# Inverse roots as exp of minus half a logarithm, with one function table on ScalarE, in a kernel of two fused transformer layers

## The reference

```python
# layer 0: attention with exponential features, then two norms, a feed-forward part and 8 experts
x = layer_norm(video + attn, g2, be2)          # (x - mu) * rsqrt(var + 1e-5)
ff = relu(x @ W1.T + b1) @ W2.T + b2
...
# layer 1: for every chunk of 64 tokens and every one of 16 heads
lr = jax.nn.sigmoid(einsum('bhkc,hcd->bhkd', xk_c, theta) + tb)
eta = token_eta * (BASE_LR * lr / HD)
Z1 = xk_c @ W + bb
std = jnp.sqrt(Z1.var(-1, keepdims=True) + EPS)
x_hat = (Z1 - mu) / std
...
Wn, bn = (W - dW, bb - db)                     # the state for the next chunk
Zq = xq_c @ Wn + bn                            # normed in the same way: std2
...
# the mixing part at the end of layer 1
r = jax.nn.sigmoid(einsum('btc,dc->btd', xr, W_r))
out = r * einsum('btc,dc->btd', square(relu(k)), W_v)
```

## Time and profile before

| what | value |
|---|---|
| median of 3 runs | 999.11 us (998.15 to 1000.2) |
| span of the profiled execution, first to last instruction | 996.6 us |
| time around the span, from the median | 2.5 us |
| PE busy | 932.1 us (94%) |
| DVE busy | 792.1 us (79%) |
| ACT busy | 659.4 us (66%) |
| POOL busy | 332.9 us (33%) |
| mean granted TensorE clock | 0.973 of full speed |

### The profile page before, as it was taken

One profiled execution on the slowest core, in us unless ns is written; L12 is line 12 of the kernel. 1 busy time (PEld: TensorE's weight loads), 2 busy tenths in 40 slices (PEclk: granted clock), 3 DMA queues, 4 the chain that ended last, 5 costly groups with the idle time before them and its releaser, 6 DMA issues.

```text
span 996.6 us, 27072 instructions
## 1 busy us (share of the span) xinstructions
PE 932.1 (94%) x10930; PEld 710.6 (71%) x10930; DVE 792.1 (79%) x1953; ACT 659.4 (66%) x1246; POOL 332.9 (33%) x434
## 2 busy tenths in 40 slices
PE   6689899999999989899999999999999998999995
PEld 5566476777777776677778776677878766777772
DVE  3845549987989778997789869897888968888873
ACT  2363346689666576698756576699766567786772
POOL 1970002225241421224342322233442334455451
PEclk9689989999999999999999999999999999999998
DMA  9000010000000010000000010000000000000000
GB/s 330 14 2 1 1 43 2 2 2 2 3 1 2 13 44 1 2 2 2 2 13 1 12 33 12 1 3 2 3 12 2 10 14 13 1 4 12 3 2 21
DMA packets 15831, 16.03 MB, mean 16 GB/s; under 512 B 2013, under 2 KB 14301, under 8 KB 15325
## 3 DMA queue, kind: packets, MB, share of 16 engines
q1 hardware_dynamic: 15709, 14.31, 4.7%
HBM read 10.12 MB, written 2.10 MB: 12 GB/s over the span
## 4 chain that ended last, share of the span: by engine, by line
PE 65%; DVE 22%; ACT 6%; issue 3%; POOL 3%; DMA 1%; ACTq 0%; SPq 0%; DVEq 0%; POOLq 0%
PE ps L532 8%; PE ps L589 5%; PE ps L595 4%; PE ps L613 4%; PE ps L525 4%; PE ps L583 4%; PE ps L572 4%; PE ps L514 3%; PE ps L481 3%; PE ps L472 3%; PE ps L398 2%; PE ps L507 2%; DVE tmp L1111 2%; POOL gbase L1312 2%; DVE tmp L1116 2%
## 5 line engine op out<-in xcount | busy, mean ns | idle before, releaser
L1312 POOL TENSOR_TENSOR gbase<-zhat,gamma 128x512 f32<-128x512 f32 x64 | 81.7, 1276 | 320.6 <-DVE scl L1105 313.1
L1320 POOL TENSOR_TENSOR zq_sqq<-zq_sqq,qinv 128x512 f32<-128x512 f32 x64 | 67.9, 1063 | 260.9 <-DVE qinv L1128 254.7
L589 PEld LDWEIGHTS ps<-grad,k_sc 64*65 64x65 f32 x2048 | 67.2, 137 | 25.0 <-issue 22.9
L772 ACT COPY w_sb<-ps 65x1024 f32<-65x1024 f32 x66 | 66.4, 1007 | 24.7 <-PE ps L589 23.6
L532 PEld LDWEIGHTS ps<-w_sb,keys 65*64 65x64 f32 x2048 | 65.6, 138 | 21.7 <-issue 12.6
L532 PE MATMUL ps<-w_sb,keys 65*64 65x64 f32 x2048 | 73.1, 224 | 6.4 <-ACT keys L780 4.8
L589 PE MATMUL ps<-grad,k_sc 64*65 64x64 f32 x2048 | 74.9, 223 | 4.2 <-DVE grad L1122 4.0
L532 PEld LDWEIGHTS ps<-w_sb,queries 65*64 65x64 f32 x2048 | 65.1, 138 | 15.2 <-issue 10.0
L532 PE MATMUL ps<-w_sb,queries 65*64 65x64 f32 x2048 | 72.6, 224 | 2.7 <-issue 1.7
L595 PEld LDWEIGHTS ps<-h,pack_ttt 128*128 128x128 f32 x512 | 64.2, 195 | 11.3 <-issue 6.4
L595 PE MATMUL ps<-h,pack_ttt 128*128 128x128 f32 x512 | 70.7, 283 | 0.2 <-ACT k_tok L800 0.2
(11 more groups left out here) (244 smaller groups left out, 2346.7 us busy)
## 6 DMA issues: line engine op xcount, KB each, us to landing
x<-in_x SPq DMA_DIRECT2D x8, 256.0 KB, 3.5
xc<-x SPq DMA_DIRECT2D x16, 128.0 KB, 2.4
out_x<-xc SPq DMA_DIRECT2D x16, 128.0 KB, 2.4
pack_ttt<-in_ttt SPq DMA_DIRECT2D x1, 1216.0 KB
keys<-in_gam_bet_rows SPq DMA_DIRECT2D x1, 1024.0 KB
w_sb<-in_compose SPq DMA_DIRECT2D x1, 1024.0 KB, 9.3
zq_sqq<-in_wmod SPq DMA_DIRECT2D x1, 768.0 KB, 4.9
pack_expert<-in_expert SPq DMA_DIRECT2D x1, 680.0 KB, 16.0
```

The lines of the kernel that those rows point to most:

```text
L589: last = mm(bank[2 * f + c][0:C, h * HD:(h + 1) * HD], k_sc[64 * c:64 * c + 64, HH * f + h, :], grad[64 * c:64 * c + 64, h, :], start=Fals ...
L772: nc.scalar.copy(w_sb[:, f, :, :, :].rearrange("p b h d -> p (b h d)"), ps[0:C, 2 * f:2 * f + 2, :].rearrange("p a c -> p (a c)")).then_in ...
L1312: P.tensor_tensor(gbase[:, cols], zhat[:, cols], gamma2[:, cols], ALU.mult).then_inc(S["g_hat"], 1)
L1320: P.tensor_tensor(heads(zq_hat[:, cols]), heads(zq_hat[:, cols]), per_head(qinv[:, hs]), ALU.mult).then_inc(S["zq_ready"], 1)
```

## The change

Every root on ACT with its reciprocal on DVE becomes two ACT instructions: a logarithm and then `exp(-0.5 * log)`, the second after a wait on the first. DVE's reciprocals of roots go, and with them the whole step `y`. The three sigmoids are made from exponentials: for `s_sig` and `eta` DVE bounds the input, ACT takes `exp(-x)`, and DVE adds 1 and takes the reciprocal; for `r_sb` ACT does four passes (relu as a bound, exp, log of 1 plus, exp). One table set that holds exp and log is loaded at the start. ACT's `v` and `w` now also wait until slot g - 2 has used `zinv` and `qinv`. Apart from `y` the strings of `ORDERS` are the same.

```diff
-    "DVE": ("111110001001001100111111000000111110011000001100r1001azbca0z0bcea1z1yazbecy0bc0a1zee1yay0bcz1bcaze11yebaycz111bc00aze1"
...
+    "DVE": ("111110001001001100111111000000111110011000001100r1001azbca0z0bcea1z1azbec0bc0a1zee1a0bcz1bcaze11ebacz111bc00aze1bce000"
...
+            nc.scalar.preload_act_table_set("natural_log_exp_and_others")
             loaded(act, "mod")
-            nc.scalar.activation(s_sig[:, :, :], cT, ACT.Sigmoid).then_inc(act_set, 1)
-            def root(name, src, dst, u=None, scale=1.0, eps=LN_EPS):
-
-                key = name if u is None else f"{name}_{u}"
-                nc.scalar.activation(dst, src, ACT.Sqrt, bias=eps, scale=scale).then_inc(S[key], 1)
+            act.wait_ge(set_step, 1)
+            nc.scalar.activation(s_sig[:, :, :], s_sig[:, :, :], ACT.Exp, scale=-1.0).then_inc(act_set, 1)
+            logs = [0]
+
+            def inverse_root(src, log, dst, sem, scale=1.0, eps=LN_EPS):
+
+                nc.scalar.activation(log, src, ACT.Ln, bias=eps, scale=scale).then_inc(S["logged"], 1)
+                logs[0] += 1
+                act.wait_ge(S["logged"], logs[0])
+                nc.scalar.activation(dst, log, ACT.Exp, scale=-0.5).then_inc(sem, 1)
...
-                nc.scalar.activation(eta[:, :, :], eta[:, :, :], ACT.Sigmoid).then_inc(S["rate_sig"], 1)
+                act.wait_ge(S["rate_bounded"], p + 1)
+                nc.scalar.activation(eta[:, :, :], eta[:, :, :], ACT.Exp, scale=-1.0).then_inc(S["rate_sig"], 1)
...
                     act.wait_ge(S["z_var"], g + 1)
-                    nc.scalar.activation(zstd[:, hs], ssum[:, hs], ACT.Sqrt, bias=TTT_EPS * HD).then_inc(S["z_std"], 1)
+                    if g >= 2:
+                        act.wait_ge(S["scale_ready"], g - 1)
+                    inverse_root(ssum[:, hs], zlog[:, hs], zinv[:, hs], S["z_inv"], eps=TTT_EPS * HD)
...
                     act.wait_ge(S["zq_var"], g + 1)
-                    nc.scalar.activation(qstd[:, hs], qsum[:, hs], ACT.Sqrt, bias=TTT_EPS, scale=1.0 / HD).then_inc(S["zq_std"], 1)
+                    if g >= 2:
+                        act.wait_ge(S["zq_ready"], g - 1)
+                    inverse_root(qsum[:, hs], qlog[:, hs], qinv[:, hs], S["zq_inv"], scale=1.0 / HD, eps=TTT_EPS)
...
-                    nc.scalar.activation(r_sb, src, ACT.Sigmoid).then_inc(drained(f"r_{n}"), 1)
+                    nc.scalar.activation(r_sb, src, ACT.Relu, bias=-LOG_LEAST).then_inc(drained(f"r_{n}"), 1)
+                    ready(act, f"r_{n}")
+                    nc.scalar.activation(r_sb, r_sb, ACT.Exp, scale=-1.0, bias=-LOG_LEAST).then_inc(S["r_step"], 1)
+                    act.wait_ge(S["r_step"], 2 * n + 1)
+                    nc.scalar.activation(r_sb, r_sb, ACT.Ln, bias=1.0).then_inc(S["r_step"], 1)
+                    act.wait_ge(S["r_step"], 2 * n + 2)
+                    nc.scalar.activation(r_sb, r_sb, ACT.Exp, scale=-1.0).then_inc(S["r_done"], 1)
...
+            link0(V.tensor_scalar(s_sig[:, :, :], cT, SIG_LEAST, None, ALU.max))
             dve.wait_ge(act_set, 1)
+            link0(V.tensor_scalar(s_sig[:, :, :], s_sig[:, :, :], 1.0, None, ALU.add))
+            link0(V.reciprocal(s_sig[:, :, :], s_sig[:, :, :]))
...
-                    dve.wait_ge(S["z_std"], g + 1)
-                    link(V.reciprocal(zinv[:, hs], zstd[:, hs]))
+                    dve.wait_ge(S["z_inv"], g + 1)
...
-                elif what == "y":
-                    dve.wait_ge(S["zq_std"], g + 1)
-                    V.reciprocal(qinv[:, hs], qstd[:, hs]).then_inc(S["zq_inv"], 1)
...
+                ready(dve, f"rate_{p}")
+                V.tensor_scalar(eta[:, :, :], eta[:, :, :], SIG_LEAST, None, ALU.max).then_inc(S["rate_bounded"], 1)
                 dve.wait_ge(S["rate_sig"], p + 1)
+                link(V.tensor_scalar(eta[:, :, :], eta[:, :, :], 1.0, None, ALU.add))
+                link(V.reciprocal(eta[:, :, :], eta[:, :, :]))
                 link(V.tensor_scalar(eta[:, :, :], eta[:, :, :], rate[:, :], None, ALU.mult))
```

More of the change, by code:

```diff
@@ L31 @@
 EPS_K, LN_EPS, TTT_EPS = 1e-4, 1e-5, 1e-6
+SIG_LEAST, LOG_LEAST = -80.0, -44.0
 NORM = DH ** -0.25
@@ L137, in turns @@
     assert all(n in (0, PAIRS * PER_TOKEN[what]) for what, n in taken.items()), taken
-PER_BATCH = [f"ln{n}_{what}" for n in range(1, 6) for what in ("var", "std", "hat")]
+PER_BATCH = [f"ln{n}_{what}" for n in range(1, 6) for what in ("var", "inv", "hat")]
 PER_BATCH += ["k_max_ready", "k_stab_ready", "k_shifted", "k_exp", "q_exp", "x_layer0"]
 PER_PAIR = [
-    "x_moved", "dve_step", "rate_sig", "w_started",
-    "w_ready", "z_squared", "z_var", "z_std", "scale_ready", "g_hat", "grad_base", "grad_ready", "k_scaled", "dw_done",
-    "zq_squared", "zq_inv", "zq_ready", "att_step", "zq_var", "zq_std", "ln6_var", "ln6_std", "ln6_hat", "mix_ready", "key_ready", "x_ttt", "x_final",
+    "x_moved", "dve_step", "rate_bounded", "rate_sig", "w_started",
+    "w_ready", "z_squared", "z_var", "z_inv", "scale_ready", "g_hat", "grad_base", "grad_ready", "k_scaled", "dw_done",
+    "zq_squared", "zq_inv", "zq_ready", "att_step", "zq_var", "ln6_var", "ln6_inv", "ln6_hat", "mix_ready", "key_ready", "x_ttt", "x_final",
+    "logged", "r_step", "r_done",
 ]
@@ L236, in build @@
         sq, tmp = sb("sq", [128, HALF]), sb("tmp", [128, HALF])
-        ssum, zstd, zinv, scl = (sb(n, [128, H]) for n in ("ssum", "zstd", "zinv", "scl"))
+        ssum, zlog, zinv, scl = (sb(n, [128, H]) for n in ("ssum", "zlog", "zinv", "scl"))
         zhat, gbase = (sb(n, [128, HW]) for n in ("zhat", "gbase"))
@@ L240, in build @@
         grad = sb("grad", [128, HH, HD])
-        qsum, qstd, qinv = (sb(n, [128, H]) for n in ("qsum", "qstd", "qinv"))
+        qsum, qlog, qinv = (sb(n, [128, H]) for n in ("qsum", "qlog", "qinv"))
         att1 = sb("att1", [128, 2, D])
@@ L763, in layer0 @@
                     act.wait_ge(S[f"{name}_var_{u}"], p + 1)
-                    root(f"{name}_std", l["mv"][:, :, 1], l["std"][:, :], u)
+                    inverse_root(l["mv"][:, :, 1], l["log"][:, :], l["inv"][:, :], S[f"{name}_inv_{u}"])
             def state0(f):
@@ L839, in mixing @@
                     act.wait_ge(S["ln6_var"], n + 1)
-                    nc.scalar.activation(std6[:, :], mv6[:, :, 1], ACT.Sqrt, bias=LN_EPS).then_inc(S["ln6_std"], 1)
+                    inverse_root(mv6[:, :, 1], log6[:, :], inv6[:, :], S["ln6_inv"])
                     if half == 0:
@@ L922, in norm_apply @@
                 l = L[u]
-                dve.wait_ge(S[f"{name}_std_{u}"], p + 1)
-                link(V.reciprocal(l["inv"][:, :], l["std"][:, :]))
+                dve.wait_ge(S[f"{name}_inv_{u}"], p + 1)
                 for t in range(T):
@@ L1150, in mixing @@
                 elif step == MIX_NORM:
-                    dve.wait_ge(S["ln6_std"], n + 1)
-                    link(V.reciprocal(inv6[:, :], std6[:, :]))
+                    dve.wait_ge(S["ln6_inv"], n + 1)
                     for j in range(4):
@@ L1168, in mixing @@
                     dve.wait_ge(S["mix_ready"], 2 * n + 2)
-                    ready(dve, f"r_{n}")
+                    dve.wait_ge(S["r_done"], n + 1)
                     V.tensor_tensor(diff_flat, filled(dve, f"val_{n}"), r_sb, ALU.mult).then_inc(drained(f"val_{n}"), 1)
@@ L1183, in _ @@
                     mixing(p, step)
-                elif what in "azbcey":
+                elif what in "azbce":
                     slot(what, p, step)
```

22 lines of the change are left out of this document (10 added, 12 removed).

## The result

The changed kernel takes 1015.63 us in the median (four runs, 1011.44 to 1023.29) against 999.28 for the kernel before (four runs): 1.0185 times as long, with a 95% interval of 1.0143 to 1.0227. The prediction, 1003.0 with a range up to 1007.5, had the sign right and a quarter of the size. The profiled execution has a span of 1009.9 us, 13.3 more than before.

The account below looks back on a forecast made before the run. It took PE as the bound, busy for 94% of the span and holding 65% of the chain. Terms summed to +4.3 us, less 0.4 for a freer DVE, taking the median from 999.11 to 1003.0 us, range 997.0 to 1007.5.

Parts of the forecast that it names:

- the sign: Whole kernel: the change makes it slower, chance 0.58, against 0.25 for the same and 0.17 for faster.
- the release of POOL's product: Product by `qinv` can run before `scl` is ready, ending a 0.04 us tie before `gbase` in seven slots: -0.3 us.
- terms for roots and for the start: Roots DVE reached late -1.5 us, three roots inside ACT runs +0.75, `eta` work before PE's first matmul +0.7, among others.
- Latency of a root: On the chain, log plus exp equals the old root plus DVE reciprocal to 0.02 us.
- Busy time: ACT some 18 us busier, near 677 us; DVE near 766; log and exp 0.21 us, an `r_sb` pass 0.60 to 0.63.
- Loads: Only eight of 33 table loads are on the chain; little to win, such as -0.3 at 244 us, -0.1 near 450.
- `eta`: Reciprocal of 0.97 us makes `eta` 1.6 us longer; `keys` near 370 us +1.8, PE waiting about 4 us; +1.2 at 593.
- `r_sb`: Mixing of the last pair: four passes start `zT` 1.15 us later at 969.82 us, and add 0.7 at 989.
- The last stretch: After 820 us: about the same 8.2 us a slot.
- Rival 4: ACT becomes a bound, +14 us on 491 in the middle; half reaching PE gives 1010 us; chance 0.03.
- The sum: All terms together +4.3 us, less 0.4 for a freer DVE in the middle: median 1003.0 us.

Follow-up runs that it names:

- e7: Kernel before, with POOL's product multiplying by `qstd` as soon as ACT has it and `y` gone from DVE: 1010.9 us, ratio 1.0097.
- e1: Changed kernel with `y` back on DVE as a copy that releases POOL's product: 1008.3 us, 1.0074 times the kernel before.
- e2: Changed kernel with POOL's product also waiting for the DVE step that stood ahead of `y`: 1010.4 us, 1.0079 times the kernel before.
- e14: Kernel before with POOL's product cut to one head of eight, by `qstd`, released by ACT, `y` kept on DVE: 998.5 us, ratio 1.0012.
- e6: Changed kernel with POOL's product held for the old DVE step, short `eta` and one-pass `r_sb`: 1003.8 us, 1.0025 times the kernel before.
- e10: Kernel before with exponentials in place of all roots and sigmoids, so no table switches: 995.0 us, ratio 0.9964.
- e4: Changed kernel with `r_sb` made in one relu pass instead of four passes: 1015.2 us, 1.0144 times the kernel before.
- e5: Changed kernel with DVE's addition and reciprocal for `eta` left out: 1016.5 us, 1.0147 times the kernel before.
- e9: Changed kernel measured again, nothing altered, beside the kernel before: 1015.9 us, ratio 1.0167.

## Why the prediction was wrong

The sign was right, and the single durations and gaps that were predicted were met or nearly so. The step that failed is the one that priced the release of POOL's product: "POOL's product by `qinv`, which now can run before `scl` is ready, ends a tie of 0.04 us in front of `gbase` in seven slots: -0.3", with the step that went before it, "taking it out is worth nothing there". Both asked who waits for `y`; neither asked what runs beside the work that `y` releases. The prediction even noted that "its product can start earlier", and saw in that only less waiting. Measured, the early release costs 9.7 us alone (e7) and gives back about 10 when it is undone (e1, e2), and e14 shows that it acts through the product's length beside DVE. A second term was too small, less surely so: the net of all its terms for roots and for the start is about +0.5, and e6 against e10 has 6 us, or some 3 at equal clock, for nearly the same things.

- **Latency of a root.** Right. In the last stretch (820 to 965 us) DVE waited 3.8 us for roots and worked 6.1 us on reciprocals; now it waits 7.4. The chain of the changed kernel near 902 us, which answers to the earlier trace rows:

```profile
901.89 0.22 ACT zlog L690
902.11 0.02 issue
902.13 0.22 ACT zinv L693
902.35 0.02 issue
902.37 0.70 DVE zhat L1122
```

- **Busy time.** Log and exp take 0.21 us and a pass 0.63, as taken. DVE is 18 us above the 766 expected: some 11 of them are the stretch by the product and 2 a stretch beside POOL's `k_sc`; the rest I have not booked.
- **Loads.** Small, as summed (e10: 3.6 us, or about 1 at equal clock).
- **`eta`.** The reciprocal takes 0.953 us (0.97 taken). At the second pair's start, all engines, answering to the earlier trace rows:

```profile
365.20 0.29 DVE L1149 TENSOR_TENSOR eta<-ps,pack_rows 128x128 f32<-128x128 f32 x1 [0.51 <-PE ps L557]
...
366.38 0.95 DVE L1154 RECIPROCAL eta<-eta 128x128 f32<-128x128 f32 x1
367.37 0.28 DVE L1155 TENSOR_SCALAR eta<-eta,rate 128x128 f32<-128x128 f32 x1
...
370.54 0.56 ACT L786 COPY keys<-ps 64x512 f32<-64x512 f32 x1
```

From DVE's first step of `eta` to `keys` it is 5.34 us where it was 3.60 (366.57, the row ahead of those in the earlier trace rows, to 370.17): +1.74, and I had +1.8. But PE waited 2.30 us for `keys` and not 4; this pair had started 1.4 us early, and that may be why.
- **`r_sb`.** ACT at the mixing of the last pair's first half, answering to the earlier trace rows:

```profile
979.87 0.63 ACT L865 ACTIVATE hat<-hat 128x512 f32<-128x512 f32 x1
980.64 0.60 ACT L867 ACTIVATE h<-ps 128x512 f32<-128x512 f32 x1
...
982.59 0.63 ACT L873 ACTIVATE h<-h 128x512 f32<-128x512 f32 x1
983.13 0.57 ACT L838 COPY zT<-ps 128x512 f32<-128x512 f32 x1
```

`zT` starts 2.63 us after the square's end and not 1.81: +0.8, where I had +1.15.
- **The last stretch.** Here the step "about the same 8.2 us a slot" fell. From `grad` of slot 48 to that of slot 63 it was 130.4 us and is 135.8. Three of DVE's operations account for 3.5 of the 5.4: in this stretch the subtraction is 0.836 us and no longer 0.700, `grad` and the `tmp` of L1134 are 0.04 longer each, 16 times. The kernel before with the early release alone (e7) takes 135.2 us for the same stretch, so the release makes 4.7 of the 5.4.
- **Rival 4** said that the middle would lose 7 us by a fuller ACT. The middle did lose 8.0, but ACT was no fuller: it was 489 us busy there and had been 491. The release makes most of it, since e7's profile loses 10.1 us between the same slots; e6 leaves room for a share of the pairs.
- **The sum.** With the release at +9.7 in place of -0.3 it would have been 1013.0, which is inside the spread of the runs. That it comes so near is partly luck, since the small terms can't be told from noise one by one. Taken out one by one, the parts give back 10 (e2), 3 (e4) and 3 us (e5), about what all three give together (15, e6); but how much of it is `eta` and how much `r_sb` stays open, since each by itself is within its interval of nothing.

## What to carry to other kernels

When a step is taken out or moved to another engine, ask what it released, and what will now run beside that. A reciprocal of 0.19 us was a gate: it held back 1.04 us of POOL's work, in most slots until DVE read PSUM or stood still. Before trusting a busy time, compare the mean of the untouched operations in both profiles: equal code on equal shapes with another duration points to contention. And a gate has two sides: opened early it cost 10 us by contention, opened late 14 us, most of it by POOL's queue.

## What was not expected of the hardware

- DVE's operations with two inputs in SBUF and POOL's product exclude each other nearly for their whole length: 0.69 and 1.04 us apart, up to 1.58 for `grad` and 1.55 for the product where they meet, and the one that began first keeps its own time. Sums over SBUF to 128x8, with one input, kept their 0.67 to 0.69 beside POOL.
- One kernel's time follows the granted clock of its run. Of 85 runs of the kernel before, the 15 at a mean clock of 0.963 to 0.965 lie at 1002.2 in the median and the 26 at 0.972 or more at 995.6; over all kernels it is 7 us for 0.01 of clock. The table's clocks differ by 0.008, which is why the small terms can't be told from it more closely. In the profile of the changed kernel TensorE was busy for 3.32 of the 5 us from 840 us, and from 845 to 850 us its granted clock was 0.50, the lower of its two levels (1.2 and 2.4 GHz), while it was busy throughout; the second profile of the changed kernel (e9) has 0.52 at the same place. Idle time alone doesn't bring it about: the kernel before was busy for 3.24 of the 5 us from 835 us and kept 1.00 through this stretch.
- POOL's product of 128x64 takes 0.31 us where 128x512 takes 1.04 to 1.06: an eighth of the elements, near a third of the time.
